# Three feed-forward tiles of the first ten sequences moved into the emptying steps of the sequence pipeline

## The reference

```
x = layernorm(x + s4d(x))          # in-projection, causal conv, long convolution by FFT, gate, out-projection
x = layernorm(x + cross(x, ctx))   # rmsnorm, 256x256 projection, plus a depooled context
x = layernorm(x + ffn(x))          # 8 experts, the best one for each token

logits = xf @ Wr.T + br                       # 1792 tokens x 8
expert_idx = argmax(logits, axis=-1)
h = relu(einsum('td,efd->etf', xf, W1) + b1)  # 256 -> 1024
y = einsum('etf,edf->etd', h, W2) + b2        # 1024 -> 256
out = y[expert_idx, arange(tokens)]
```

## Time and profile before

| what | us |
|---|---|
| median of 3 runs (lowest, highest) | 363.5 (362.51, 364.04) |
| the profiled execution | 362.94 |
| its span, first to last instruction | 361.1 |
| busy: TensorE, VectorE, ScalarE, GpSimd | 326.5, 213.3, 151.5, 204.1 |
| mean granted TensorE clock | 0.952 |

### The profile page before, as it was taken

How to read it: one execution, slowest core, us unless ns; L and a number is a source line. 1 busy time by engine, 2 the same in 40 slices (tenths; PEclk the granted TensorE clock), 3 DMA queues, 4 the chain that set the end, 5 groups by cost and what they waited for, 6 DMA issues and landing times.

```text
span 361.1 us, 6567 instructions
## 1 busy us (share of the span) xinstructions
PE 326.5 (90%) x1910; PEld 258.0 (71%) x1911; DVE 213.3 (59%) x478; ACT 151.5 (42%) x383; POOL 204.1 (57%) x335
## 2 busy tenths in 40 slices
PE   7999999998999999999985239999999999999970
PEld 3455555566787777877863229999999999999950
DVE  5999995347777788788853541334443444344430
ACT  3888853445354434534452112342234323432320
POOL 4789970246766877687743060254464556454642
PEclk9999999999999999999997557999999999999995
DMA  6910004203655665564530862011001010101110
GB/s 179 362 28 4 0 0 128 86 26 104 183 187 158 182 172 178 157 172 154 156 116 14 319 244 90 9 37 45 31 21 41 26 44 15 44 22 37 31 44 22
DMA packets 17847, 34.92 MB, mean 97 GB/s; under 512 B 3504, under 2 KB 9527, under 8 KB 17176
## 3 DMA queue, kind: packets, MB, share of 16 engines
q1 hardware_dynamic: 15224, 29.88, 26.5%
q0 software_dynamic: 1872, 4.59, 4.3%
q10 hardware_dynamic: 720, 0.08, 0.2%
HBM read 30.87 MB, written 4.20 MB: 97 GB/s over the span
## 4 chain that ended last, share of the span: by engine, by line
PE 76%; DVE 13%; issue 4%; POOL 3%; ACT 1%; DMA 1%; ACTq 1%; POOLq 0%; DVEq 0%
PE ps L1496 19%; PE ps L1514 17%; DVE stage_b L992 9%; PE ps L1422 8%; PE ps L1402 7%; PE ps L1281 5%; PE ps L1446 4%; PE ps L1330 4%; PE ps L1331 4%; PE ps L1450 2%; PE ps L1483 1%; PE ps L1457 1%; PE ps L1411 1%; DMA stage_b<-x_rows,stage_b 1%; PE ps L1435 1%
## 5 line engine op out<-in xcount | busy, mean ns | idle before, releaser
L1496 PEld LDWEIGHTS ps<-stage_b 128*128 128x128 f32 x576 | 69.5, 198 | 2.6 <-DVE stage_b L1195 1.0
L1496 PE MATMUL ps<-stage_b 128*128 128x128 f32 x576 | 69.9, 281 | 1.2 <-ACT stage_b L935 1.2
L1514 PE MATMUL ps<-w,stage_b 128*128 x288 | 65.4, 379 | 1.2 <-issue 1.2
L1514 PEld LDWEIGHTS ps<-w,stage_b 128*128 128x128 f32 x288 | 53.3, 190 | 8.3 <-issue 1.8
L1083 DVE TENSOR_TENSOR stage_b<-ps,w 112x512 f32<-112x512 f32 x64 | 39.7, 684 | 14.4 <-PE ps L1331 12.3
L926 ACT ACTIVATE stage_b<-ps,b 128x128 f32<-128x128 f32 x144 | 39.1, 382 | 7.3 <-issue 7.3
L935 ACT ACTIVATE stage_b<-ps 128x256 f32<-128x256 f32 x19 | 7.3, 383 | 82.6 <-PE ps L1483 82.6
L651 POOL TENSOR_TENSOR stage_b<-stage_b 112x512 f32<-112x512 f32 x16 | 21.6, 1348 | 34.9 <-DVE stage_b L1083 22.8
L706 POOL DMA_INDIRECT stage_b<-x_rows,stage_b x21 | 32.1, 1529 | 8.4 <-issue 6.0
L1402 PEld LDWEIGHTS ps<-consts,stage_b 112*128 112x128 f32 x256 | 31.0, 192 | 7.1 <-issue 6.6
L1195 DVE COPY stage_b<-w 128x2048 f32 x19 | 23.7, 1250 | 20.8 <-issue 14.0
(11 more groups left out here) (172 smaller groups left out, 541.7 us busy)
## 6 DMA issues: line engine op xcount, KB each, us to landing
w<-in_w SPq DMA_DIRECT2D x16, 512.0 KB, 4.1
w<-in_w SPq DMA_DIRECT2D x16, 256.0 KB
w<-in_w SPq DMA_DIRECT2D x4, 1024.0 KB
stage_b<-in_ctx SPq DMA_DIRECT2D x16, 224.0 KB, 3.0
w<-in_x_t SPq DMA_DIRECT2D x4, 448.0 KB, 7.0
stage_b<-in_x SPq DMA_DIRECT2D x16, 112.0 KB, 3.2
x_rows<-stage_b SPq DMA_DIRECT2D x16, 112.0 KB, 1.9
shared<-in_b SPq DMA_DIRECT2D x1, 1024.0 KB, 4.9
```

The lines of the kernel that those rows point to most:

```text
L1496: last_ = m.matmul(ps[:, 2 * par + f // 4, (f % 4) * P:(f % 4 + 1) * P], w1_now[par][:, k, f * P:(f + 1) * P], rows_t[:, par, k * P:(k + 1 ...
L1514: last_ = m.matmul(ps[:, 4 + par, 0:D], h_t[:, par, f * P:(f + 1) * P], w2[:, e, f, :], start=(f == 0), stop=(f == FT - 1))
```

## The change

Three tiles of the main stage are computed earlier, out of tokens of the first ten sequences alone. Group 2 ends with sequence 9; once it is ranked (`RANKED` is now one step earlier for every group), totals of ten sequences give each expert's full tiles (`early_experts`, step 14), and the first three of them, in the experts' order, are the early tiles. `early_tokens` (step 15) marks the tokens in them and gives the others their places without them; `tokens_early` (TensorE, step 16) makes their token numbers; GpSimd gathers their rows from a second table `x2_early` in step 16; SyncE loads w1 and w2 of the first two experts in step 15 and of the third in steps 18 and 19, into space of the w2 slots 4 and 5 and of stage B's spectrum buffers, so the main loads of w2 4 and 5 wait for the early products. TensorE's steps 16 to 19 are written out in a new order: `turn_early` (transposes), `hide_early(i, part)` (half of the first product), `sum_up_early(i, part)` (half of the second product) stand between the steps' own work, and the last token products behind the first product of the third tile. ScalarE moves the rows and makes the relus, VectorE and GpSimd the norms, in the first two main steps; then GpSimd scatters the three tiles. The main stage has three tiles less, and its loop runs twice instead of three times.

The diff, cut to its core:

```diff
-RANKED = (9, 13, 15, 19)
+RANKED = (8, 12, 14, 18)
+EARLY, EARLY_SEQS, EARLY_GROUP = 3, 10, 2
...
-            groups = (TPE + 2 - F_PRO) // F_UNROLL
+            groups = (TPE - EARLY + 2 - F_PRO) // F_UNROLL
...
@@ SyncE: step @@
+                    if b < EARLY_SEQS:
+                        sp.dma_start(x2_early[bass.ds(b * L, L), :], x2[:, par, :]).then_inc(early_stored[par], 16)
+                if 2 * pair + q == NB + 2:
+                    sp.wait_ge(ht_e_ps, 2)
+                    load_early_w1(2)
+                if 2 * pair + q == NB + 3:
+                    sp.wait_ge(f_e_ps, 1)
+                    load_early_w2(2)
+                if b == NB - 1:
+                    sp.wait_ge(expert_e_set, 1)
...
+                    for i in range(2):
+                        load_early_w1(i)
+                        load_early_w2(i)
-            for e in (4, 5, 7, 6):
+            for e in (7, 5, 4, 6):
+                if e in (4, 5):
+                    sp.wait_ge(ht_e_ps, 6 if e == 4 else 4)
@@ GpSimd: step (before the root of sequence s - 2), and main steps 0 and 1 @@
+                if 2 * pair + q == NB:
+                    pool.wait_ge(token_e_set, 1)
...
+                    gather_early(0)
+                    gather_early(1)
...
+                if 2 * pair + q == NB:
+                    gather_early(2)
...
+                    for n in range(EARLY):
+                        g.indirect_dma_start(out, bass.IndirectOffsetOnAxis(
...
@@ ScalarE @@
+            def relu_early(i, part):
+                act.wait_ge(y_set, NB)
+                act.wait_ge(expert_e_set, 1)
+                e = act.value_load(expert_e[0:1, i:i + 1], min_val=0, max_val=NE - 1)
+                act.wait_ge(ht_e_ps, 2 * i + part + 1)
...
@@ VectorE: step, and the main stage's start @@
+                if s == RANKED[EARLY_GROUP]:
+                    early_experts()
+                if s == RANKED[EARLY_GROUP] + 1:
+                    early_tokens()
...
             take_w1(0, 0)
+            measure_early(0)
+            measure_early(1)
...
@@ TensorE @@
+            def turn_early(i):
+                pe.wait_ge(rows_e_loaded, 16 * EARLY)
+                pe.wait_ge(pre_set, NB)
+                need(pe, rt_e_set, i)
+                for k in range(DT):
+                    last_ = m.transpose(ps[:, 4, D + k * P:D + (k + 1) * P], rows_e[:, i, k * P:(k + 1) * P], ident)
+                last_.then_inc(rt_e_ps, 1)
+            def hide_early(i, part):
+                pe.wait_ge(w1_e_loaded[i % 2], 16 * (i // 2 + 1))
+                pe.wait_ge(rt_e_set, i + 1)
...
+            def sum_up_early(i, part):
+                pe.wait_ge(w2_e_loaded[i % 2], 16 * (i // 2 + 1))
+                pe.wait_ge(ht_e_set, 2 * i + part + 1)
...
+                    if s == NB:
+                        tokens_early()
...
+                if s == NB + 1:
+                    project(NB - 1)
+                    turn_x1(NB - 2)
+                    turn_early(0)
+                    turn_x2(NB - 3)
+                    hide_early(0, 0)
+                    cross(NB - 2)
+                    logit(NB - 3)
+                    hide_early(0, 1)
+                if s == NB + 2:
+                    turn_x1(NB - 1)
+                    sum_up_early(0, 0)
+                    turn_x2(NB - 2)
+                    cross(NB - 1)
+                    rank_group(RANKED.index(s))
+                    logit(NB - 2)
+                    sum_up_early(0, 1)
+                    turn_early(1)
+                    hide_early(1, 0)
+                if s == NB + 3:
+                    turn_x2(NB - 1)
+                    hide_early(1, 1)
+                    logit(NB - 1)
+                    sum_up_early(1, 0)
...
+            sum_up_early(1, 1)
+            turn_early(2)
+            hide_early(2, 0)
+            hide_early(2, 1)
             pe.wait_ge(parts_set, 2)
             for b in range(NB):
...
+            sum_up_early(2, 0)
+            sum_up_early(2, 1)
```

More of the change, by code:

```diff
@@ new lines, in turn_x2, with cross @@
+            def turn_x2(b):
+                par = b % 2
+                pe.wait_ge(x2_set, b + 1)
+                need(pe, x2t_set, b)
+                need(pe, logit_set, b)
+                for k in range(DT):
+                    last_ = m.transpose(ps[:, 7, k * L:(k + 1) * L], x2[:, par, k * P:(k + 1) * P],
+                                        ident[0:L, 0:L])
+                last_.then_inc(x2t_ps, 1)
+            def cross(b):
+                par = b % 2
+                pe.wait_ge(x1t_set, b + 1)
+                pe.wait_ge(gains_set, DT + 1)
+                pe.wait_ge(z_set, UNITS)
+                need(pe, sum2_set, b)
+                for k in range(DT):
+                    m.matmul(ps[0:L, 6, 0:D], x1_t[:, par, k * L:(k + 1) * L], w_x[:, k, :],
+                             start=(k == 0), stop=False)
+                pe.wait_ge(u_set, b + 1)
+                pe.wait_ge(decay_kept, b + 1)
+                m.matmul(ps[0:L, 6, 0:D], decay_b[:, par, :], u[:, par, :], start=False, stop=True)\
+                 .then_inc(cross_ps, 1)
```

305 lines of the change are left out of this document (236 added, 69 removed).

## The result

The changed kernel takes **358.97 us** (median of 4 runs, 358.64 to 360.29) beside 363.77 us for the kernel before in the same rounds (4 runs, 362.51 to 365.31). The ratio is 0.9873, 95% interval 0.9826 to 0.9919. The change gains 4.8 us; the forecast was 9.

A forecast was written before the change was run, and what follows sets the result against it. TensorE was taken as the bound from about 230 us, with a chain of latencies before. Terms -21.7 + 9.8 + 2.5 + 0.4 = -9.0 us on 362.94 gave 354.0 us; forecast range 351.5 to 358, wider range 348.5 to 361.

The forecast's parts named there:

- Removed tiles: Main stage: three of 18 tiles leave, at 7.245 us each, for -21.7 us.
- First and second: Steps 14 to 16: expert list makes the inverse transform 2.3 us late; token parts make sequence 14's projection 3.4 us late.
- Third: Early gathers: third issued from 191.5, landing 3.1 us later at 194.7; TensorE waits for it, early weights no bound.
- Fourth: TensorE from 194.8: early tiles among the steps' own work; last token products end at 222.45, 12.4 us late.
- Fifth: Start of main stage: gather lands 3.85 us behind token products; second main product at 232.2, +9.8 us.
- Sixth: Clock: one fall while TensorE is idle from 191.1 to 194.8, 5.3 us at the lower level, +2.5 us.
- The copy on VectorE: Start of main stage: VectorE's weight copy, behind two early means, ends at 232.2 and sets the second main product.
- At nothing: Costs taken as nothing: ten further stores, early norms and scatters in main steps 0 and 1; nested end test 0.4 us.
- hand-offs cost more: Emptying steps: ScalarE's register loads stand open and gathers land later than 3.1 us; 358 to 361 us, chance 0.18.
- ScalarE's register loads: Emptying steps: taken as 0 under TensorE's wait, at most five times 1.06 us.
- The slower rival: Emptying steps, TensorE from 194.8 to 226: clock stays low throughout, 373 us; chance 0.08.
- the rule of the Trainium skill: Emptying steps: short bursts of products with waits between start each at the lower clock, so every wait pays 2.5 us.

The follow-up runs named there:

- e7: Changed kernel with the w2 load of expert 4, like expert 6's, held until the first main gather landed: 354.22 us, ratio 0.9758.
- e1: Changed kernel with w1 and w2 of the second early tile loaded only after the three early gathers landed: 356.16 us, ratio 0.9828.
- e6: Changed kernel plus 26 unused products on ones ahead of the first early tile's transposes: 357.25 us, ratio 0.9770.
- e11: Changed kernel with third early gather beside the first two, second early tile's weights behind early gathers, w2 of experts 4 and 6 behind main gather: 349.89 us.
- e2: Changed kernel with all four last w2 loads held until the first main gather landed: 362.51 us, ratio 0.9999.
- e3: Changed kernel plus ten unused products on ones ahead of the main stage's first transposes: 355.59 us, ratio 0.9830.
- e10: e7 run again, in the same rounds as the changed kernel: 354.15 us, ratio 0.9761.
- e9: The changed kernel run again without edits: 357.77 us, ratio 0.9862.
- e12: e11 plus unused products on ones in step 17, ten before sequence 14's transposes, seven before the first early tile's: 348.06 us, ratio 0.9600.
- e8: Changed kernel with the edits of e1, e3 and e7, and the third early gather issued with the first two: 351.91 us, ratio 0.9665.

## Why the prediction was wrong, step by step

The direction held, and so did the mechanism of the gain, three tiles less in the main stage; the growth of the emptying steps was sized too small. The start of the second main product moved by 17.9 us (222.39 to 240.29), where the sum had 9.8 + 2.5 = 12.3. By the steps of the prediction, on the profile of the changed kernel:

| step | forecast | measured | us late, in all |
|---|---|---|---|
| third early gather issued | 191.5 | 192.29 | +0.8 |
| its landing | 3.1 us | 5.71 us | +3.3 |
| first early transposes to the end of the last token products, with 2.5 for the clock | 30.15 | 28.05 | +1.1 |
| end of token products to the second main product | 9.75 | 14.19 | +5.6 |
| second main product to the end | 119.2 | 118.4 | +4.8 |

- **Removed tiles.** Right: 22.2 us, forecast 21.7 less 0.4, at the same pitch of 7.24 us (first products at 327.47 and 334.71).
- **First and second.** Right in the chain: inverse transform forecast near 181.0, measured 180.62. The projection of sequence 14 ended at 188.1 and not at 186.0, since the clock fell here in this execution; e7, without the fall, issued the third gather at 190.95.
- **Third.** Wrong in one term. The price of 3.1 us came from a row whose DMA engines were 23% busy; 4 MB of early weights stood ahead of this gather (share 0.99 just before it). e1 took half of the loads away and got 3.30. The sentence that the early weights are no bound looked only at the product that reads them. The transfer beside them paid. As a rival it was named, without a price. Most of this loss did not reach the end of the token products (+1.1 there).
- **Fourth.** Too dear: 28.05 us, forecast 27.65 and 2.5 for the clock; the fall at 194.5 cost about 1.2 (3.01 us for 2.02 in the half product, 0.69 for 0.44 in the transposes, both beside e6 and e11), and some waits were shorter.
- **Fifth.** This is the step that failed. The sum took 3.85 us for the main gather behind the token products (3.08 of it the transfer) and 3.8 for the first main product at the full clock. Measured were 4.80 us for the transfer alone and 6.71 for the product: 1.7 + 2.9 us, nearly the whole of the miss of 4.8. The change itself moves the main load of w2 of expert 4 behind the third early product, a moment ahead of this gather; the sum put that at nothing and gave no reason. e2 and e7 show the first part to be the w2 loads issued just ahead; e3 removes the second without the first; e7 removes both by one line of order and takes 354.22 and, again as e10, 354.15 us. From the end of the token products to the second main product e7 takes 9.32 us, where the sum had 9.75 and the changed kernel took 14.19.
- **Sixth.** Wrong in number: the clock fell three times in this profile. "A second fall of the clock" stood among the signs of a wrong prediction, and it was there. The price was taken from the last 5.3 us of a low stretch; in the kernel before the granted clock is 0.50 from 193.4 to 220.6 us.
- **The copy on VectorE** (232.2), which was to set the second main product, is no bound: it ended at 234.7, and the first main product at 239.5 (at 235.7 in e9).
- **At nothing.** Stores, early norms and the nested test: the last term of the table is 0.8 us shorter than the sum, so none of them shows.

The time fell where the rival "hand-offs cost more" had it (358 to 361), by a cause like that rival's second, late gathers, but at the main gather and with the clock behind it, which the rival did not name; that the number fits is luck. Two of the ten executions of the changed kernel, 354.70 and 354.74 us, came within 0.8 us of the forecast; in the profiled one of them the clock stayed up ahead of the main stage. ScalarE's register loads, its first, are not among the long waits of the chain. The slower rival, the clock low throughout, didn't come: from 201.2 to 231.8 the clock is 1.00. With the rule of the Trainium skill behind it (page "TensorE: Matmul & The Clock Gate", section "HAM oscillation — how this bites in real kernels") the trace agrees in part: three of the stops were followed by the lower clock (0.50 to 0.52 in the windows above), though not every one, and not in every execution.

## What to carry to other kernels

A transfer's duration from a trace is its price beside the loads of its own window: read the DMA share there, and look at what the change puts on the same DMA engines at the new time, above all large loads that nothing hurries. A short stop of TensorE ahead of a stage is paid twice where the clock falls in it, so order the loads such that the small transfer on the chain comes first, and hold back only as many as the next reader can spare (here two of the four loads instead of one gained 2.4 to 3.6 us in the same rounds, while all four gave the gain of the change back: ratio 0.9999). Where two executions of one program differ by 4 us, profile both before explaining the median, and compare two profiles from a point ahead of the edit on: two of the profiles here were late by 1.8 to 1.9 us before it.

## What was not expected of the hardware

- The first main gather took 2.82 to 3.29 us in the five profiles with expert 4's load behind it (e2, e7, e10, e11, e12) and 3.87 to 6.12 in the seven with that load just ahead (the changed kernel, e1, e3 to e6, e9). Among the seven the DMA share does not order it: 4.80 us at 0.68 (the changed kernel), 3.87 at 0.82 (e9).
- The same stop of TensorE with the same instructions around it was followed by the lower clock in some executions and not in others (3.57 and 2.04 us above; five of twelve).
- Products on ones into an unused bank kept the clock at its upper level through a wait for a transfer (e3, e6). They were hidden as long as they ended before it landed, and stood on the chain with 2.16 us when they didn't (e8).
